# Second attention of a macaron block: scores in halves of two PSUM banks, stacks of blocks 1 to 3 by way of DRAM

## What is computed

```python
x = x + 0.5 * moe_top2(ln(x))          # L0_ffn: 8 experts and a shared one
x = x + linear_attention(ln(x))        # L0_attn: 4 blocks
x = x + 0.5 * moe_top2(ln(x))          # L0_ffn again
x = x + 0.5 * expert_choice(ln(x))     # L1_ffn: each expert takes its best 64 tokens per sequence
x = x + causal_attention(ln(x))        # L1_attn: the part that changes
x = x + 0.5 * expert_choice(ln(x))     # L1_ffn again
```

```python
q, k, v = split(x @ W_attn + b_attn)              # 16 heads of 8
att = einsum('bhqd,bhkd->bhqk', rope(q), rope(k)) / sqrt(8)
att = softmax(where(causal, att, -inf))
return (att @ v) @ W_proj + b_proj
```

## Time and profile before

| | us |
|---|---|
| median of 3 runs (1082.54 to 1086.08) | 1083.9 |
| profiled execution, its own time | 1078.49 |
| its span, first to last instruction | 1076.8 |
| mean granted TensorE clock | 0.925 |

### The profile page before, as it was taken

The page is one execution under the profiler, slowest core; times in us unless marked ns, Lnnn a source line. Parts: engine busy times, 40 slices in busy tenths (PEclk is TensorE's granted clock), DMA queues, the critical chain, the costliest instruction groups (busy, mean ns, idle before and its releaser), DMA issues.

```text
span 1076.8 us, 13026 instructions
## 1 busy us (share of the span) xinstructions
PE 933.8 (87%) x4507; PEld 628.2 (58%) x4507; DVE 708.1 (66%) x1413; ACT 619.6 (58%) x1003; POOL 337.8 (31%) x249
## 2 busy tenths in 40 slices
PE   6899999579999999879999997799967777777997
PEld 4678887123333333337788876488644545455886
DVE  3978887467778777646788886744276556547532
ACT  6555555268888888863555555544554545455454
POOL 1597777000000000001677775201201221123200
PEclk8999999689999999997999998699988778888999
DMA  5125110000000000003311110200000000001001
GB/s 172 43 79 159 66 62 27 0 1 0 1 1 1 0 1 0 1 0 118 76 64 64 64 50 16 63 21 2 1 0 3 4 2 2 4 1 39 1 2 40
DMA packets 30743, 33.64 MB, mean 31 GB/s; under 512 B 2062, under 2 KB 19798, under 8 KB 30678
## 3 DMA queue, kind: packets, MB, share of 16 engines
q1 hardware_dynamic: 30678, 32.81, 9.9%
HBM read 31.36 MB, written 1.18 MB: 30 GB/s over the span
## 4 chain that ended last, share of the span: by engine, by line
PE 61%; DVE 19%; ACT 11%; issue 4%; POOL 3%; DMA 0%; ACTq 0%; SPq 0%; DVEq 0%; POOLq 0%
PE ps L128 10%; PE ps L129 10%; PE ps L130 10%; PE ps L750 5%; PE ps L862 4%; PE ps L744 2%; ACT ex L1485 2%; PE ps L955 2%; PE ps L728 2%; ACT L1374 2%; POOL fl L2155 2%; DVE smax L2034 1%; PE ps L891 1%; PE ps L964 1%; PE ps L736 1%
## 5 line engine op out<-in xcount | busy, mean ns | idle before, releaser
L2155 POOL TENSOR_TENSOR fl<-fp,fh 128x512 fp32r<-128x512 f32 x144 | 223.5, 1568 | 126.3 <-ACT fh L1280 126.0
L1271 ACT ACTIVATE fs<-ps 128x512 f32<-128x512 f32 x144 | 86.2, 599 | 114.6 <-PE ps L130 114.4
L1743 DVE TENSOR_TENSOR fp<-fp,cwb 128x512 f32<-128x512 f32 x128 | 141.2, 1103 | 14.0 <-DVE fp L1736 0.9
L1736 DVE TENSOR_TENSOR fp<-fs,ps 128x512 f32<-128x512 f32 x144 | 98.2, 682 | 40.7 <-ACT fs L1271 40.1
L128 PE MATMUL ps<-z_hi,w_hi 128*128 128x512 f32 x288 | 117.0, 406 | 3.3 <-DVE fp L1736 3.3
L129 PE MATMUL ps<-z_lo,w_hi 128*128 128x512 f32 x288 | 116.6, 405 | 0.0
L130 PE MATMUL ps<-z_hi,w_lo 128*128 128x512 f32 x288 | 115.0, 399 | 0.0
L1280 ACT CAST fh<-fp 128x512 fp32r<-128x512 f32 x144 | 88.8, 617 | 36.8 <-DVE fp L1743 32.6
L2219 POOL TENSOR_TENSOR ln_sq<-ln_rs 128x512 f32<-128x512 f32 x20 | 21.1, 1056 | 272.4 <-ACT ln_rs L1337 272.4
L2212 POOL TENSOR_SCALAR_AFFINE_SELECT ex<-ex 128x1024 f32<-128x1024 f32 (+1 forms) x24 | 33.4, 1403 | 152.4 <-ACT ex L1485 152.4
L2034 DVE TENSOR_REDUCE smax<-ps 128x8 f32<-128x2048 f32 (+1 forms) x24 | 55.0, 2291 | 38.8 <-PE ps L969 31.9
(11 more groups left out here) (270 smaller groups left out, 2005.2 us busy)
## 6 DMA issues: line engine op xcount, KB each, us to landing
cwb<-cw_spread SPq DMA_DIRECT2D x64, 256.0 KB, 3.1
w_raw<-in_L_ffn_w_dram SPq DMA_DIRECT2D x20, 256.0 KB, 2.9
w_raw<-in_L_ffn_w_dram SPq DMA_DIRECT2D x4, 512.0 KB, 5.9
w<-in_L_ffn_w_dram SPq DMA_DIRECT2D x8, 256.0 KB, 4.4
x_tok<-in_L_attn_x_dram SPq DMA_DIRECT2D x4, 256.0 KB, 3.5
wb<-in_L_attn_W_dram SPq DMA_DIRECT2D x1, 1024.0 KB, 7.0
wb<-in_L_attn_W_dram SPq DMA_DIRECT2D x4, 256.0 KB, 4.0
out_dram<-z SPq DMA_DIRECT2D x4, 256.0 KB, 3.0
```

Of the source, the lines that this page charges most:

```text
L1271: act.activation(fs[:, n % 2, :], ps[:, n % 2, :], ACT.Silu).then_inc(silu_done, 1)
L1736: dve.tensor_tensor(f, fs[:, n % 2, :], ps[:, 2 + n % 2, :], ALU.mult).then_inc(prod_done, 1)
L1743: dve.tensor_tensor(f, f, cwb[:, x % CW_RING, :], ALU.mult).then_inc(weighed, 1)
L2155: pool.tensor_tensor(fl[:, n % RING0, :], fp[:, n % RING0, :], f32(fh[:, n % RING0, :]), ALU.subtract).then_inc(flo_done, 1)
```

## The change

1. Plain and turned scores are made in six halves of two banks each (`PLAIN`, `TURNED`, with their banks); DVE takes six maxima of 1024 columns per sequence in place of three, ACT six exponentials in place of three. The order of the pieces on PE, ACT and POOL is new, and so are the banks of the other results.
2. Block 0 is stacked as before. For blocks 1 to 3, `project_both` makes q and k of a block unstacked, 128 features each (weights `wun`, bias `bsu`); ACT writes the high part (`both_high`, into `hm`), DVE the low part (`both_low`, into `low_qk`).
3. SP's `load_stack` stores both to DRAM (`qk_rows`), waits until they have landed, and for blocks 2 and 3 until the stack to be overwritten is no longer read, and loads 24 pieces (q and k, three parts, four heads g) of 8 partitions by 4 by 512 into the stack; for blocks 2 and 3 two loads of zeros clear the rows of the maxima. For block 1, POOL clears that stack before the rounds and sets the rows that are one. `load_stack` stands on SP's queue behind the placing of sequences 0, 2 and 4, and PE waits for all its loads (`rows_loaded`) before the block's first plain scores.

```diff
+        PLAIN = ((1, 0), (1, 1), (0, 0), (0, 1), (2, 0), (2, 1))
+        PLAIN_BANK = (0, 2, 0, 2, 0, 2)
+        TURNED = ((2, 0), (2, 1), (0, 0), (0, 1), (1, 0), (1, 1))
+        TURNED_BANK = (6, 6, 4, 4, 6, 4)
+        PART_HALF = ((0, 0, 1), (0, 1, 0))
...
+        def rows_loaded(tb):
+            return 16 * (4 * PARTS * 2 * tb + 2 * (tb - 1))
...
+            def load_stack(tb):
+                for half, (done, t) in enumerate(((high_done, hm), (low_done, low_qk))):
+                    sp.wait_ge(done, 2 * tb)
+                    sp.dma_start(qk_dram[:, half].rearrange("n p t -> p n t"), f32(t[:])).then_inc(qk_stored, 16)
+                sp.wait_ge(qk_stored, 32 * tb)
+                if tb == 1:
+                    sp.wait_ge(blank_done, 1)
+                else:
+                    sp.wait_ge(t_ready, 6 * (SPB * tb - 2))
+                    for h in range(2):
+                        sp.dma_start(f32(stk[tb % 2][ROW_MAX + h:ROW_MAX + h + 97:32, 0, :, :]), no_max[h * HEADS:(h + 1) * HEADS, :]).then_inc(stk_loaded, 16)
+                for n in range(2):
+                    for k in range(PARTS):
+                        src = qk_dram[n, PART_HALF[n][k]].rearrange("(h g r) t -> g r h t", h=HG, g=4)
+                        for g in range(4):
+                            r0 = 32 * g + HD * k
+                            sp.dma_start(f32(stk[tb % 2][r0:r0 + HD, n, :, :]), src[g]).then_inc(stk_loaded, 16)
...
+                if s in (0, 2, 4):
+                    load_stack(s // 2 + 1)
...
+                def project_both(tb, n):
+                    mm3(pe, ps[:, qk_bank(tb, n), :], wun_hi[:, n, :], wun_lo[:, n, :], blk(z_hi, tb), blk(z_lo, tb)).then_inc(both_ready, 1)
...
+                def both_high(tb, n):
+                    act.wait_ge(both_ready, 2 * (tb - 1) + n + 1)
...
+                    act.activation(hm[:, n, :], ps[:, qk_bank(tb, n), :], ACT.Identity, bias=bsu[:, n:n + 1]).then_inc(high_done, 1)
...
+                def exps(s, i):
+                    act.wait_ge(t_ready, 6 * s + i + 1)
+                    n, j = TURNED[i]
+                    bank = TURNED_BANK[i]
+                    act.activation(ex[:, s % 2, n, 2 * j:2 * j + 2, :].rearrange("p g t -> p (g t)"),
+                                   ps[:, bank:bank + 2, :].rearrange("p g t -> p (g t)"), ACT.Exp, scale=SCALE).then_inc(exp_done, 1)
...
+                def both_low(tb, n):
+                    dve.wait_ge(high_done, 2 * (tb - 1) + n + 1)
...
+                    dve.scalar_tensor_tensor(out=low_qk[:, n, :], in0=ps[:, qk_bank(tb, n), :], scalar=bsu[:, n:n + 1],
+                                             in1=f32(hm[:, n, :]), op0=ALU.add, op1=ALU.subtract).then_inc(low_done, 1)
```

PE's new order in a round, with its main waits (lines on the next layer left out):

```diff
+                        if s < 1:
+                            pe.wait_ge(stk_done, 2 * HG)
+                        else:
+                            pe.wait_ge(stk_loaded, rows_loaded((s + 1) // SPB))
...
+                        plain(s + 1, 0)
...
+                        plain(s + 1, 1)
...
+                        turned(s, 0)
+                    if summed:
+                        pe.wait_ge(exp_done, 6 * s)
...
+                        outputs(s - 1, (0, 1))
+                        plain(s + 1, 2)
+                        turned(s, 1)
+                        plain(s + 1, 3)
...
+                        outputs(s - 1, (2, 3)).then_inc(o_ready, 1)
+                        plain(s + 1, 4)
+                        turned(s, 2)
+                        plain(s + 1, 5)
+                        flip(s - 1)
...
+                        turned(s, 3)
...
+                        turn(tb - 1)
+                        maxima(s + 1)
...
+                        values(tb + 1)
+                        project_both(tb + 2, 0)
+                        turned(s, 4)
+                        project_out(tb - 1)
...
+                        project_both(tb + 2, 1)
+                        turned(s, 5)
+                        values_turned(tb + 1)
```

More of the change, by code:

```diff
@@ L1079, in attn1 @@
                     if s < 0:
-                        project_in(1, range(2))
+                        for n in range(2):
+                            project_both(1, n)
                     if s == SEQS - 1:
-                        ln_variance(LN_FFN1B, 0)
-                        ln_variance(LN_FFN1B, 1)
-                    if second and tb >= 1:
-                        project_out(tb - 1)
-                    if s == SEQS - 1:
-                        scores(LN_FFN1B, 0)
-                        scores(LN_FFN1B, 1)
@@ L1100, in attn1 @@
-                    if second and more:
-                        pe.wait_ge(vaug_done, tb + 2)
-                    if first and more:
-                        pe.wait_ge(stk_done, (tb + 1) * 2 * HG + stack_mid(tb + 1) + 3)
-                    if s + 1 < SEQS:
-                        maxima(s + 1)
-                    if s < 0:
-                        for k in range(2, 4):
-                            pe.wait_ge(stk_done, 2 * HG + k - 1)
-                            project_in(1, (k,))
-                    if second and tb >= 1:
-                        pe.wait_ge(ln_in, u0 + NTB + tb)
@@ L1126, in attn1 @@
-                    if first and more and tb > 0:
-                        pe.wait_ge(exp_done, 3 * s + 2)
-                        project_in(tb + 1, range(4, 8))
-                    if s == SEQS - 1:
-                        pe.wait_ge(exp_done, 3 * s + 2)
                         for t in range(SPB):
@@ L1504, in attn1 @@
                     more = tb + 1 < NTB
-                    if 0 <= s < SEQS:
+                    soft = 0 <= s < SEQS
+                    if soft:
                         exps(s, 0)
-                    if second and more:
-                        values(tb + 1)
-                    if second and tb >= 1:
-                        turn(tb - 1)
                     if s == SEQS - 1:
@@ L2083, in attn1 @@
                         part_weights(1, LN_FFN1B, 0)
-                    if s >= 1:
-                        normalise(s - 1)
-                    if first and more and tb > 0:
-                        stack(tb + 1, range(4, 8))
+                    if second and tb >= 1:
+                        low(tb - 1)
+                    if 0 <= s and second and tb + 2 < NTB:
+                        both_low(tb + 2, 0)
+                    if second and tb >= 1:
+                        add(tb - 1)
+                    if 0 <= s and second and tb + 2 < NTB:
+                        both_low(tb + 2, 1)
+                    if second and more:
+                        values(tb + 1)
+                    if s < 0:
+                        for n in range(2):
+                            both_low(1, n)
                     if s == SEQS - 1:
@@ L2198, in attn1_masks @@
                 pool.sem_inc(cmask_done, 1)
+                own.did(pool.memset(no_max[:], 0.0))
+                pool.wait_ge(z_ready, NTB * HALVED.index(LN_ATTN1) + NTB)
+                own.did(pool.memset(f32(stk[1][:, 0]), 0.0))
+                own.wait()
+                own.did(pool.tensor_scalar(stk[1][:, 1], f32(stk[1][:, 0]), rope[:, HG * P + 2:HG * P + 3], None, ALU.add))
+                own.wait()
+                pool.sem_inc(blank_done, 1)
                 for v in vaug:
```

284 lines of the change are left out of this document (149 added, 135 removed).

## The result

The median is 1125.8 us (4 runs, 1118.69 to 1133.22) against 1083.7 us for the kernel before (4 runs, 1082.54 to 1086.08): 1.039 times as long, with a 95% interval of 1.030 to 1.047. I had forecast 1075, in a range of 1060 to 1091. The change makes the kernel slower, and the time is outside the range.

What follows compares the result with a forecast made beforehand. No engine was taken as full; a chain of waits from engine to engine bounds the kernel. Load paths, shorter rounds and clock additions summed to `turn` at 963.4, -9 us: 1083.9 - 9 = 1075, range 1060 to 1091.

Steps and rivals of the forecast that it cites:

- three paths from `low_done` to scores: Stores, loads and landing before rounds 1, 3, 5: 4.3 + 13.4 + 1.3 = 19.0 us for block 1, 20.2 for blocks 2 and 3.
- The loads: SP's stack loads per block: issued 0.56 us apart, 24 taking 13.4 us, 26 taking 14.6, the last landing 1.3 later.
- The result that I drew from the page, 1061: Case of the 20% cheap-loads rival with transfers, not issue, as the bound: paths 4 to 5 us shorter per block, about -23.
- The stores: SP's 512 KB stores to DRAM: 4.3 us from `low_done`, between the rows for 256 KB and 1024 KB.
- Clock: After PE idles 5 to 9 us before rounds 1, 3, 5: 1.5 us added to each, and 2 to round 6.
- Halves: Scores in halves: exponential 1.01 us, maximum 1.25, PE's products 0.8 or 0.45; plain round 11.8 us, odd 13.3 at full clock.
- the rival of cheap loads (-26): Stack loads at 0.34 us each, so shorter waits before rounds 1, 3, 5: -26 us, 1058; chance 20%.
- The loads are dear: Rival: stack loads 0.83 us apart, 76 issues costing 20.5 us more in all: +11.5, 1095; chance 15%.
- the clock doesn't return: Rival: restarted rounds run at 1.2 GHz to their end, 5.5 us more in each of three: +7, 1091; chance 8%.
- the rounds stay long: Rival: doubled hand-offs keep plain rounds at 14.4 us, odd ones 3 longer: about 1084, no change; chance 17%.
- signs for a wrong main term: Profile checks on the stack loads: spacing above 0.68 us, or PE not waiting for them, would show the main term wrong.
- Priced at nothing: Terms counted as zero, among them POOL's added column in `stk`, covered up to 11 us before DVE wants `vaug`.

Runs made afterwards that it cites:

- step3: Kernel after, each of the 24 loads per block writing every third partition instead of 8 neighbours: 1108.1 us, 1.020 times the kernel before.
- image_all: Kernel after, stacks loaded by two 1 MB DMAs onto 128 partitions, unused products in three waits before round 0 and 12 ahead of rounds 1, 3, 5: 1066.8 us.
- the bare pair: Kernels before and after, each without making the stacks of blocks 1 to 3 (block 0's stack reused): 1071.7 us with whole pieces, 1063.0 with halves.
- image_start: Kernel after, stacks loaded by two 1 MB DMAs onto 128 partitions, unused products only in three waits before round 0: 1074.3 us.
- image_odd: Kernel after, stacks loaded by two 1 MB DMAs onto 128 partitions, 12 unused products only ahead of rounds 1, 3 and 5: 1064.0 us, 0.982 times before.

## Why the prediction was wrong

All terms, with the 8.0 us ahead of the stage taken off (us; after from PE's and DVE's timelines, `low_done` at 821.50, 871.53 and 923.08, the ends of these):

```profile
820.75 0.75 DVE L2099 SCALAR_TENSOR_TENSOR low_qk<-ps,bsu,hm 128x512 fp32r<-128x512 f32 x1 [0.53 <-ACT hm L1526]
...
870.78 0.75 DVE L2099 SCALAR_TENSOR_TENSOR low_qk<-ps,bsu,hm 128x512 fp32r<-128x512 f32 x1 [0.74 <-ACT hm L1526]
...
922.33 0.75 DVE L2099 SCALAR_TENSOR_TENSOR low_qk<-ps,bsu,hm 128x512 fp32r<-128x512 f32 x1 [0.62 <-ACT hm L1526]
```

| step | forecast | after | more |
|---|---|---|---|
| `low_done` of block 1 | 808.6 | 813.5 | 4.9 |
| three paths from `low_done` to scores | 19.0, 20.2, 20.2 | 30.6, 31.4, 31.7 | 34.3 |
| rounds 1 and 3, to `low_done` | 17.0, 17.3 | 19.4, 20.1 | 5.2 |
| round 5 | 14.8 | 18.1 | 3.3 |
| round 6 | 13.8 | 13.1 | -0.7 |
| rounds 7 and 8, to `turn` | 32.5 | 34.6 | 2.1 |

That is 49.1 us. With 8.0 ahead of the stage and 5.0 behind it, it makes the 62 us between the 1069.5 that I forecast for a profiled execution and 1131.6. Behind the stage PE ran at a granted clock of 0.88, where it was 0.94.

**The loads: the step that failed.** I priced a load by its issue, 0.56 us, and took 1.5 MB in 10.5 us from the row of a 1 MB load onto all 128 partitions. The issue was dearer in my sum than on the chip (0.34). But the transfer takes 26.6 us, 2.5 times those 10.5, and it sets the wait: from the first issue to the scores I had 14.7. My bounds were bounds of issue, 0.34 to 0.83, and the transfer stood in the text as a side line that could only make loads cheaper. No row of before had a load onto 8 partitions, which I wrote myself; the honest bound from the rows had no upper end for that. Contiguous source, stepped destination, 24 and 128 partitions show that the destination was the cause.

The Trainium skill (DMA: Bandwidth & Descriptors, "Issuing engines are not separate DMA queues") had issue small beside the DMA itself; I held rows against it. The trace after agrees with the page: 8.2 of 26.6 us. In step3 the issue was the larger part, 16.8 of 18.8. The result that I drew from the page, 1061, took the transfer to be short, so that rival fell as well.

**The stores** were right: 3.2 us for `hm` and 3.9 for `low_qk`, and 4.0 from `low_done` to the first load, where I had 4.3.

**Clock.** I gave 1.5 us to each restarted round, from a 4 us recovery after 5 us of idle time. That row is one of 128x512 products. The halves' short products ran 6 to 9 us at 1.2 GHz in after, 14.5 and 19.2 with 24-partition loads, and 14.5 without loads, with hardly an idle time ahead. Products like those behind the idle time in my row are what the change takes out of the rounds. The odd rounds begin at 1.2 GHz, and the first scores of sequence 0 fall to it at 804.9. How much of the 8.5 us in rounds 1, 3 and 5 is clock is shown by image_all's profile, where they run at 2.4 GHz: 16.6 and 17.1 us to `low_done` and 15.3 for round 5, where my sum at full clock had 15.5, 15.8 and 13.3. So 4.4 us are rounds that are longer at full clock too, among them by the dearer half scores (below); the clock cost 8.6 us in the three rounds, 4.1 above my 4.5. The 4.9 before `low_done` aren't divided. Fills gave back less than I expected each time: 2.7 us ahead of round 1, 7.6 of 16 in the odd rounds, 10 of 18 to 26 in the waits. The rest stays open; so does why recovery took 9 us after a wait of 20 us, and 14.5 to 19.2 after waits of 6 to 8.

**Halves.** 1.01 and 1.25 us a piece were right for ACT and DVE (1.02, 1.22). PE's term was mis-sized: I took half of a whole piece, 0.8 us for a half with the triangle and 0.45 for the others. In round 6 they took 1.13 and 0.76 to 0.85, since a half's products took as long as a whole piece's. So a plain round at full clock took 13.1 us (round 6), not 11.8 (the 13.8 in the table hold 2.0 for the clock); PE was busy for 8.65 of its first 9.07 us, so waits weren't the reason there. The 14.4 before were at a granted clock of 0.81. By the bare pair halves gain 8.7 us.

**What there was to win.** I let -9 come out of a sum of many terms without asking for its ceiling. Without any making of stacks the kernel before is 12 us faster, and halves on top give 8.7: 21 us in all, as long as the path by DRAM costs nothing. At the clock that these runs were granted, the rival of cheap loads (-26) was thus out of reach for this reason alone.

**The rivals.** None had this mechanism. "The loads are dear" gave 1095 by a spacing that wasn't there; "the clock doesn't return" gave 1091, and was part of it, as was "the rounds stay long" (odd rounds 2.4 to 3.3 us above my sum). My own signs for a wrong main term looked at the spacing and not at the rate: it was below 0.68 and PE did wait, so they would have let it pass. Of what I said would show, only the length of the wait failed, 18 to 20 us for 5 to 9, and the spacing, 0.34 for 0.56. Priced at nothing and hidden indeed: POOL's column, 5.45 us (bound 11).

## What to carry to other kernels

Price a DMA by what it writes to, not only by bytes and issues: 64 KB onto 8 neighbouring partitions took over 1 us each in a queue, while 1 MB onto 128 landed 7.4 us (median) after its issue. Before trading PE work for transfers, leave that work out in a run: the ceiling was 12 us here, and the clock over the stage fell with it from 0.83 to 0.73. Before cutting a piece in two, see how many of its products ran side by side: here half a piece cost PE as much as a whole one. Where PE must wait, a few dense products that end just as the data land can be worth more than idling: 8 to 11 us here, with loads of 24 and of 128 partitions. It is no rule: fills ahead of the first scores raised the clock and gained nothing, with halves (1074.3 against 1075.3) as with whole pieces (1082.4), and why isn't shown.

## What the runs showed of the hardware that I had not expected

- Rate of the loads by destination: 64 GB/s (8 neighbours), 171 (24 neighbours), 300 (128).
- A load onto every third partition is issued in 0.70 us, one onto neighbours in 0.34.
- A contiguous 64 KB source made no difference (62 GB/s against 64).
- Rounds of the same products ran for 102.6 us at 2.4 GHz behind a fill of 12 products (image_all), and the first of them for 15.0 us at 0.52 without it (image_start), with PE busy 92.3 of 102.6 us in the one and 14.6 of 15.0 in the other. In image_odd's profile the clock fell again after 19 us.
- Four score products of 32x256 of two heads took 0.50 us, eight of four heads 0.52.
